# First edge stage of a four-layer graph network: middle layer feature-major, last layer's weights applied per edge block

## What is computed

```python
h = jnp.maximum(_layernorm(x), 0.0)
r = edge_index[1]                                   # destination
c1ij = jnp.concatenate([x[r], edge_attr], axis=1)   # here x is h; 64 + 64 features
h = softplus(c1ij @ W1 + b1)                        # 128 wide
h = softplus(h @ W2 + b2)                           # 128 wide
out = h @ W3 + b3                                   # 64 wide
agg = segment_sum(out, r, num_segments=x.shape[0])
```

## Time and profile before

| | |
|---|---|
| median of 3 runs | 10330.74 us |
| the profiled execution | 10343.41 us, its span 10341.8 us |
| stage changed, from its first `selT` to its last `add` | 144 us to 1605 us of the span |
| PE busy over the span | 5765.4 us (56%) |
| PE weight loads | 3576.5 us (35%) |
| DVE busy | 4372.1 us (42%) |
| ACT busy | 2424.1 us (23%) |
| POOL busy | 6918.9 us (67%) |

### The profile page before, as it was taken

How to read it: one execution, slowest core, us unless ns; L and a number is a source line. 1 busy time by engine, 2 the same in 40 slices (tenths; PEclk the granted TensorE clock), 3 DMA queues, 4 the chain that set the end, 5 groups by cost and what they waited for, 6 DMA issues and landing times.

```text
span 10341.8 us, 144754 instructions
## 1 busy us (share of the span) xinstructions
PE 5765.4 (56%) x32026; PEld 3576.5 (35%) x32026; DVE 4372.1 (42%) x11981; ACT 2424.1 (23%) x4618; POOL 6918.9 (67%) x7939
## 2 busy tenths in 40 slices
PE   6999996244444447999999962333333322222222
PEld 4777773222222223444444432222222211111111
DVE  6888886132323225777777751111111111111111
ACT  5999993000000002333333320000000000000000
POOL 3333331777777776777777757777777677777777
PEclk9999998555555558999999985555555555555555
DMA  3333333111111112222222211111111111111111
GB/s 104 96 97 96 97 97 118 27 29 30 29 30 29 30 29 51 61 61 61 61 61 60 60 37 27 28 28 28 28 28 28 24 27 28 28 28 28 28 28 27
DMA packets 503888, 488.54 MB, mean 47 GB/s; under 512 B 245340, under 2 KB 299425, under 8 KB 503777
## 3 DMA queue, kind: packets, MB, share of 16 engines
q0 software_dynamic: 220480, 235.58, 11.9%
q1 hardware_dynamic: 283360, 252.43, 8.4%
HBM read 427.04 MB, written 61.15 MB: 47 GB/s over the span
## 4 chain that ended last, share of the span: by engine, by line
POOL 46%; PE 26%; issue 18%; DVE 5%; ACT 1%; POOLq 1%; DVEq 1%; DMA 0%; ACTq 0%; SPq 0%
POOL mov L671 44%; PE ps L1527 5%; PE ps L1416 3%; PE ps L1390 3%; PE ps L1423 3%; PE ps L1519 3%; POOL outs L671 2%; PE ps L1546 1%; DVE scr L940 1%; PE ps L1512 1%; PE ps L1508 1%; PE ps L1537 1%; PE ps L1414 1%; PE ps L1452 1%; PE ps L1430 1%
## 5 line engine op out<-in xcount | busy, mean ns | idle before, releaser
L1390 PE MATMUL ps<-outs,mov 128*64 128x64 f32 x9984 | 1370.5, 319 | 4220.3 <-DMA mov<-tab_q,idx 1616.3
L1390 PEld LDWEIGHTS ps<-outs,mov 128*64 128x64 f32 x9984 | 1158.2, 221 | 4548.1 <-issue 4548.1
L840 DVE TENSOR_TENSOR acc<-acc,ps 64x64 f32 (+1 forms) x1664 | 354.1, 213 | 4441.8 <-PE ps L1390 4439.5
L671 POOL DMA_INDIRECT mov<-tab_msg,idx x1664 | 1578.6, 949 | 665.7 <-issue 492.3
L671 POOL DMA_INDIRECT outs<-tab_u,idx x1664 | 1590.2, 956 | 582.1 <-issue 486.4
L671 POOL DMA_INDIRECT mov<-tab_h,idx x1664 | 1573.9, 946 | 574.8 <-issue 506.6
L671 POOL DMA_INDIRECT mov<-tab_q,idx x1664 | 1573.3, 945 | 543.1 <-issue 506.6
L940 DVE TENSOR_TENSOR scr<-ps,scr 128x512 f32<-128x512 f32 x1664 | 1063.1, 685 | 368.9 <-PE ps L1519 337.3
L1527 PE MATMUL ps<-scr,w_bas 128*64 128x512 f32 x3328 | 899.9, 619 | 0.0
L634 POOL TENSOR_TENSOR scr<-outs 128x128 f32<-128x128 f32 x416 | 191.8, 461 | 816.3 <-DVE outs L850 815.5
L850 DVE TENSOR_TENSOR outs<-rel,iota_w 128x256 f32<-128x256 f32 x1664 | 705.6, 424 | 43.1 <-issue 30.1
(11 more groups left out here) (217 smaller groups left out, 8426.4 us busy)
## 6 DMA issues: line engine op xcount, KB each, us to landing
mov<-in_dst_row SPq DMA_DIRECT2D x832, 128.0 KB, 2.7
mov<-in_ea_T SPq DMA_DIRECT2D x416, 128.0 KB, 2.5
tab_msg<-outs SPq DMA_DIRECT2D x104, 256.0 KB, 2.0
mov<-tab_msg,idx POOLq DMA_INDIRECT x1664
outs<-tab_u,idx POOLq DMA_INDIRECT x1664
mov<-tab_h,idx POOLq DMA_INDIRECT x1664
mov<-tab_q,idx POOLq DMA_INDIRECT x1664
win<-tab_g SPq DMA_DIRECT2D x416, 32.0 KB, 2.4
```

Of the source, the lines that this page charges most:

```text
L671: nc.gpsimd.indirect_dma_start(out=gat(e, u)[:, k, :], out_offset=None, in_=table, in_offset=bass.IndirectOffsetOnAxis(ap=idx[:, u, k:k + ...
L840: nc.vector.tensor_tensor(into, into, bank(banks[u % len(banks)])[0:rows, 0:W], ALU.add) \
L1390: last = mm(bank(banks[u % len(banks)])[0:width, 0:W], values(u)[:, k, :], sel(e, u)[:, k, :], start=k == 0, stop=k == TL - 1)
```

## The change

The second layer is made feature-major, one matmul with `w_l0m` stationary and the 512 edges moving. The bias then lies along partitions, one value each, in `b_l0m` [128,1]; DVE's clip and maximum add it as a per-partition scalar. The third layer is applied to each block of 128 edges before the sum over edges (`mm3`, four matmuls with a `hid2` block stationary and the 65 columns of `w_l0o` moving). ACT's `move` copies these 4 x 65 columns. `to_acc` sums them per node: four matmuls with `moved` blocks stationary and `sel` moving. `moved` goes from its own buffer to a free part of the ring memory. The split of the bias, its trip through DRAM and its matmul go.

```diff
-            (r_b, t["L0_b2"]), ...
+            (b_l0m[:, :], t["L0_b2"].rearrange("a d -> d a")), ...
...
-            sp.wait_ge(bias_split, 1)
-            for a in range(3):
-                sp.dma_start(bias_parts[a:a + 1, :], r_parts[a]).then_inc(bias_rt, 16)
-            sp.wait_ge(bias_rt, 48)
-            sp.dma_start(bpart[:, :], bias_parts[:, :]).then_inc(bias_rt, 16)
...
-                order(nc.vector.tensor_copy(r_parts[0], r_b))
-                order(nc.vector.tensor_tensor(r_bd, r_b, r_parts[0], ALU.subtract))
-                order(nc.vector.tensor_copy(r_parts[1], r_bd))
-                nc.vector.tensor_tensor(r_parts[2], r_bd, r_parts[1], ALU.subtract).then_inc(bias_split, 1)
...
+                def soft2_stage(it, u, _):
+                    dve.wait_ge(softened2, done_of(2, g, it, u, 1))
+                    dve.wait_ge(hid_summed, done(g, it, u, 2))
+                    nc.vector.scalar_tensor_tensor(out=hid2[:, u % 2, :], in0=bank(2 + u % 2), scalar=b_l0m[:, 0:1],
+                                                   in1=soft2[:, u % 2, :], op0=ALU.add, op1=ALU.max) \
+                        .then_inc(hid2_ready, 1)
+
+                def clip2(it, u, _):
+                    dve.wait_ge(mm2_done, done(g, it, u))
+                    dve.wait_ge(hid2_ready, done(g, it, u, 2))
+                    nc.vector.tensor_scalar(soft2[:, u % 2, :], bank(2 + u % 2), b_l0m[:, 0:1], CLIP, ALU.add, ALU.min) \
+                        .then_inc(clipped2, 1)
...
-                    nc.scalar.activation(moved[:, u % 2, :], bank(4 + u % 2)[:, 0:W], ACT.Copy).then_inc(hid_moved, 1)
+                    nc.scalar.activation(moved[:, u % 2], bank(4 + u % 2)[:, 0:TL * (D + 1)].rearrange("p (k c) -> p k c", k=TL),
+                                         ACT.Copy).then_inc(hid_moved, 1)
...
+                def mm3(it, u, _):
                     pe.wait_ge(hid2_ready, done(g, it, u))
+                    pe.wait_ge(hid_moved, done(g, it, u, 2))
+                    out_ = bank(4 + u % 2)[:, 0:TL * (D + 1)].rearrange("p (k c) -> p k c", k=TL)
+                    for k in range(TL):
+                        last = mm(out_[:, k, :], hid2[:, u % 2, k * P128:(k + 1) * P128], w_l0o[:, :],
+                                  start=True, stop=True)
+                    last.then_inc(hid_summed, 1)
 
                 def mm2(it, u, _):
                     pe.wait_ge(hid1_ready, done(g, it, u))
                     pe.wait_ge(hid2_ready, done(g, it, u, 2))
-                    out_ = bank(2 + u % 2).rearrange("p (k c) -> p k c", k=TL)
-                    mm(out_, ones_b[:, :], bpart[:, :].unsqueeze(1).to_broadcast([3, TL, H]), start=True, stop=False)
-                    for k in range(TL):
-                        last = mm(out_[:, k, :], hid1[:, u % 2, k * P128:(k + 1) * P128], w_l0m[:, :],
-                                  start=False, stop=k == TL - 1)
-                    last.then_inc(mm2_done, 1)
+                    mm(bank(2 + u % 2), w_l0m[:, :], hid1[:, u % 2, :], start=True, stop=True).then_inc(mm2_done, 1)
...
                     mm(out_, b_l0o[:, :], sel_sum[:, u % SL, :], start=True, stop=False)
-                    mm(out_, w_l0o[:, :], moved[:, u % 2, :], start=False, stop=True).then_inc(agg_done, 1)
+                    for k in range(TL):
+                        last = mm(out_, moved[:, u % 2, k, :], sel(0, u)[:, k, :], start=False, stop=k == TL - 1)
+                    last.then_inc(agg_done, 1)
 
                 chunk_loop(pe, [
-                    (1, mm1), (3, mm2), (6, to_acc),
-                    (5, sum_stage(0, p, H, lambda u: hid2[:, u % 2, :].rearrange("p (k c) -> p k c", k=TL),
-                                  hid2_here, (4, 5), hid_summed))])
+                    (1, mm1), (3, mm2), (6, to_acc), (5, mm3)])
```

More of the change, by code:

```diff
@@ L62, in build_gnn @@
         basis_parts = dram("basis_parts", [3, NBAS * CH * CE], BF16)
-        bias_parts = dram("bias_parts", [3, H], BF16)
         x = sb("x_nodes", [P128, NB, D])
@@ L84, in build_gnn @@
         ones = sb("ones", [P128, P128])
-        ones_b = sb("ones_b", [3, P128], BF16)
         eps_c = sb("eps_c", [P128, 1])
@@ L114, in build_gnn @@
         bas = sb("bas", [P128, SL, CE], BF16)
-        moved = sb("moved", [H, 2, W])
         pair = sb("pair", [P128, NBAS, P128], BF16)
@@ L122, in build_gnn @@
         soft1, hid1, soft2, hid2 = (ring2(n) for n in range(4))
+        moved = ring_mem[:, 12 * CE - P128:12 * CE - P128 + 2 * TL * (D + 1)].rearrange("p (s k c) -> p s k c", s=2, k=TL)
         sel_half = ring_mem[:, 8 * CE:8 * CE + 4 * W].rearrange("p (s k c) -> p s k c", s=2, k=2)
@@ L172, in build_gnn @@
         b_c2 = sb("b_c2", [1, 2 * D])
-        bpart = sb("bpart", [3, H], BF16)
+        b_l0m = sb("b_l0m", [P128, 1])
         b_ii1 = sb("b_ii1", [P128, 1])
@@ L180, in build_gnn @@
         r_pib2 = raw[0:1, 8 * D:9 * D]
-        r_b, r_bd = raw[0:1, 9 * D:11 * D], raw[0:1, 12 * D:14 * D]
         r_w3 = outs[0:D, 0, :]
         b_rz = outs[0:D + 1, 2, 0:2 * D]
-        r_parts = [outs[0:1, 1, n * D:(n + 1) * D].bitcast(BF16) for n in range(3)]
         PW = NBAS * CH * CE // (P128 * ITERS)
@@ L204, in build_gnn @@
         folded = sem("folded")
-        bias_split = sem("bias_split")
-        bias_rt = sem("bias_rt")
         ints_loaded = sem("ints_loaded")
@@ L423, in build_gnn @@
             (r_pp2b, t["pp_b2"]), (r_pib1, t["pi_b1"]), (r_pib2, t["pi_b2"]),
-            (r_b, t["L0_b2"]), (b_ii1[0:D, :], t["ii_b1"].rearrange("a d -> d a")), (b_ii1[D:P128, :], t["ii_b1"].rearrange("a d -> d a")),
+            (b_l0m[:, :], t["L0_b2"].rearrange("a d -> d a")), (b_ii1[0:D, :], t["ii_b1"].rearrange("a d -> d a")), (b_ii1[D:P128, :], t["ii_b1"].rearrange("a d -> d a")),
         ]
@@ L428, in build_gnn @@
         ALL_LOADED = 16 * (len(LOADS) + 1)
-        N_CONSTS = 27
+        N_CONSTS = 26
         block = ctx.enter_context(nc.Block())
@@ L589, in _ @@
                                  allow_small_or_imprecise_dtypes=True))
-            for tile_, value in ((ones[:, :], 1.0), (ones_b[:, :], 1.0), (eps_c[:, :], EPS),
+            for tile_, value in ((ones[:, :], 1.0), (eps_c[:, :], EPS),
                                  (hT[D:P128, :, :], 0.0), (w_typ[D:P128, :], 0.0), (w_l0n[D:P128, :], 0.0), (hT[D:D + 1, :, :], 1.0),
@@ L902, in edge_mlp @@
                 return [(3, soft_of_size),
-                        (4, clip(mm2_done, hid2_ready, clipped2, soft2, 2)),
-                        (5, soft(hid2_ready, softened2, hid_summed, None, soft2, hid2, 2)),
+                        (4, clip2), (5, soft2_stage),
                         (0, selT_stage(0, p, slice(D, P128), 3)),
@@ L1349, in _ @@
             last.then_inc(folding, 1)
-            pe.wait_ge(bias_rt, 64)
             for flow, _, _ in FIRST_STORED:
@@ L1405, in _ @@
                 g = pe.snap(p * CH)
-                def hid2_here(it, u):
+                def mm3(it, u, _):
                     pe.wait_ge(hid2_ready, done(g, it, u))
+                    pe.wait_ge(hid_moved, done(g, it, u, 2))
[4 more added lines that the diff above has]
+                    last.then_inc(hid_summed, 1)
                 def mm2(it, u, _):
```

## The result

The changed kernel takes 10384.14 us, the median of 6 runs (10380.95 to 10384.64), the kernel before beside it 10330.74 (10329.4 to 10331.79), the median of five runs. A sixth run of the kernel before, 1.7% longer (10509.86), was in the chip's slower state and is left out. The ratio is 1.0051, 95% interval 1.0039 to 1.0062: slower by half a per cent, some 53 us. 10390 was forecast.

What follows compares the result with a forecast made beforehand. PE's list bound the kernel at 3.45 us a step; afterwards a three-engine loop would. 416 x (0.11 + 0.03) = +58, with +1 once, makes +59 us: 10402 profiled, 10390 against the median; range 10338 to 10428.

Steps and rivals of the forecast that it cites:

- The bound of before: Edge stage before the change: PE's own list sets the pace at 3.45 us a step; ACT and the loop are hidden.
- The floor of ACT's list: ACT alone in the edge stage: 3.23 us a step before, 3.39 after the wider move.
- The loop: Path through ACT, DVE and PE over two steps: 7.125 us after the change, 3.56 a step, becoming the bound.
- The signs that I named: Expected trace: PE waits for DVE's maximum and add in most steps, near 3.6 us each; ACT waits 0.1 to 0.2.
- mm2 and mm1: PE's first- and second-layer matmuls, 0.90 us each with a float32 successor, from 2.32 together to 1.80.
- The lower bound of 0.85: Lower bound in us for a 512-column matmul on PE, given as 1024 columns at 2.4 GHz.
- What was covered: Disturbed selT on DVE, 550 ns mean against 490, hidden behind PE before: adds 0.03 us a step, 0 to 0.06.
- Once: One-time effects outside the steady steps: layer-norm fold at most 1 us, draining +2, filling about 0.5 shorter; sum +1.
- ACT in full: Rival: ACT's wait stays, so the step grows by the move's whole 0.163 us; +68 us, 10399; chance 0.18.
- Dearer weights: Rival: a matmul pair in to_acc costs 0.22 us, 0.20 a step more; +83 further, 10473; chance 0.03.
- no change: Rival: free scalars, no extra 0.05 at to_acc, cheaper move; 3.47 us a step, +8 us, 10339; chance 0.08.
- faster: Rival: the loop never closes and ACT alone binds at 3.39 us a step; -25 us, 10306; chance 0.09.

Runs made afterwards that it cites:

- e7: Kernel before without its one bf16 matmul, the middle layer's bias, which is left out; 10295.3 us, ratio to the kernel before 0.9954.
- e4: Kernel before with ACT's move writing its 64 columns four times, 256 columns, PE using the first copy; 10345.7 us, ratio to before 1.0013.
- e8: Kernel before with ACT's move writing 256 columns and DVE's add first in its list; 10335.8 us, ratio to before 0.9993.
- e5: Changed kernel with DVE's add first in its list and PE's to_acc ahead of mm2; 10265.5 us, ratio to the kernel before 0.9925.
- e1: Changed kernel with DVE's add of the sums moved from last to first in its list; 10345.2 us, ratio to the kernel before 1.0013.
- e3: Changed kernel with clip and maximum in their old forms, the middle layer's bias left out; 10363.3 us, ratio to the kernel before 1.0031.
- e2: Changed kernel with one of the four matmuls of moved blocks in to_acc; 10327.0 us, ratio to the kernel before 0.9994.
- e9: Kernel before with DVE's add first in its list and PE's to_acc ahead of mm2; 10293.6 us, ratio to before 0.9963.

## Why the prediction was right

*The bound of before.* Right: e7 shows PE's list binding, e4 and e8 that ACT had room for nearly all of 0.16 more. The floor of ACT's list was put too high: its last instruction gives way to the move after 0.53 at the least in the changed kernel, so ACT alone comes to 3.29, not 3.39; e5, in which ACT hardly ever waits, runs at 3.300.

*The loop.* Right in place and size: 7.15 for 7.125. Within it, errors of some hundredths cancel. The clip and the maximum cost 62 and 63 ns, not 45 and 50, and 0.06 each to the next start; L1411 starts 0.31 after the add, not 0.26; to_acc is 0.14 + 0.48, not 0.64; the move takes 385 ns where 387 were forecast, and gives way after 0.29 instead of 0.30. e1 shows the wait for the add, e3 the scalars, e2 the four pairs as members of the loop. The signs that I named came out in part. PE waits for the maximum and for the add, but clearly only in every second step, and so steps of 3.86 and 3.29 alternate, which I had not seen; ACT waits 0.28 a step in the mean, more than the 0.1 to 0.2 forecast.

*mm2 and mm1.* Taken at 0.90. Where nothing was waited for, mm1 gave way to mm2 after 0.91, and mm2 to to_acc after 0.86 at the earliest. mm2 itself starts 0.89 after the start of the maximum that it waits for (1633.83 to 1634.72), where I had 0.84. The lower bound of 0.85 has no sum behind it as it stands: 1024 columns at 2.4 GHz are 0.43, half of it.

*What was covered.* Sized about right, by luck, since the cause was the wrong one. I added 0.03 for the disturbed `selT`; but after the change its mean is 493 ns, nearly undisturbed, because POOL's instruction now starts 0.44 before it and is nearly through (888.13 and 888.57). The 3.575 of the loop and the 3.615 of the mean differ by 0.04. The most of it is that in each turn of eight chunks one pair takes 7.42 in place of 7.15 (moves at 884.12, 887.48, 891.54), at the turn's end. There DVE's L879 starts 0.83 after ACT's L1200 and not 0.66, which is 0.17 of the 0.27; `selT` takes 0.52, so it is not `selT`. What holds L879 back was not found.

*Once.* Filling was mis-sized: the first move comes 5.7 us earlier, where I had 0.5. Of that, 0.7 is the layer norm's (L752 at 58.65 where L768 stood at 59.34), as I said of the fold; the rest is the filling and was not tested apart. e4, which has the fold and mm2 of before, also has its first move 3 us earlier (158.4), so not all of it need be the change's.

*The rivals.* 'ACT in full' has a time near the measured one and falls by e1, which leaves ACT's list as it is and takes 39 us away, and by e4. The rule of the Trainium skill, Perfetto Trace Analysis, section Identifying the Most-Contended Engine, names the most occupied engine as the one to optimize first, here ACT. The trace does not bear it out: ACT waited for mm3 115 us in all, 0.28 a step, and e5 frees 130 us without touching ACT. An edit of ACT alone was not run; its move, Abs and Exp stand in the loop too. 'Dearer weights' falls by the pairs' 0.12, 'no change' and 'faster' by the result.

## What to carry to other kernels

When several engines are nearly full, write down the loops that pass through more than one engine's list before shortening the fullest one; the second-longest loop is what is left after the change. Look in such a loop for an instruction that stands in it only by its place in a list: here two moves of a line turned 0.5% slower into 0.75% faster. A cost of 0.35 us inside a loop of two steps is paid by half (e2: 0.36 off the undisturbed pair of steps). And ask what an earlier engine will run into: in e2 and e3 a part of the gain was lost in the one step of each turn in which DVE met POOL.

## What the runs showed of the hardware

The clip, with the per-partition scalar added, took DVE 742 ns on 128x512, where it took 680 before; e3 gives the 62 ns back. For the maximum a part of the 63 is the form: `soft_of_size`, also a three-operand instruction but with an immediate, takes 692, the maximum with a per-partition scalar 743; by these two the scalar itself costs some 51 ns. Both delay the next start by 0.06.

A 512-column float32 matmul pair gave way after 0.86 to 0.93 us to a float32 successor and after 1.01 to a bf16 one. The eight float32 matmuls of `sum_stage` or mm3 gave way to mm1 after 0.89 or 0.90 with to_acc in front of them and after 0.84 with mm2 in front (e5, e9).

A `selT` takes 0.485 to 0.490 us in the kernel before whenever no instruction of POOL is beside it (314 of 416). Beside POOL's 0.67 us one it took 0.97 when both started together (e7 at 895.28, and 50 times in the kernel before), 0.90 when POOL's was 0.05 ahead (e2 at 889.51) and 0.52 when it was 0.44 ahead (the changed kernel at 888.57). When `selT` was first, POOL's took 0.93 and `sel` behind it 0.78 instead of 0.43, in e8:

```profile
890.11 0.49 DVE L860 TENSOR_SCALAR mov<-mov,node_of 64x512 f32<-64x512 int32 x1
...
890.19 0.93 POOL L624 TENSOR_TENSOR scr<-scr 128x256 bf16<-128x256 f32 x1
...
890.63 0.78 DVE L850 TENSOR_TENSOR outs<-rel,iota_w 128x256 f32<-128x256 f32 x1
```

By these figures the two don't share; the one that comes second waits until the other is nearly through. The Trainium skill, GPSIMD Engine Reference, section 1, Specifications, says that GpSimd's SBUF interfaces are shared with VectorE, with contention for DVE instructions in a two-port performance mode or with two SBUF inputs. `sel` has two SBUF inputs, and the trace agrees with its 0.78; in which mode `selT` runs no row shows.
